# Softmax pass of a graph network: value minus last maximum by a second turning and a matmul with a negated identity on PE, in place of DVE's difference

## The reference, cut to what matters

```python
m = jax.nn.relu(feat[src]) + EPS
logits = BETA * m
seg_max = jax.ops.segment_max(logits, dst, num_segments=N)
ex = jnp.exp(logits - seg_max[dst])
denom = jax.ops.segment_sum(ex, dst, num_segments=N)
a = ex / denom[dst]
msg = jax.ops.segment_sum(a * m, dst, num_segments=N)
feats = feat + msg
return feats @ W + b
```

## Time and profile before

| | us |
|---|---|
| median of 3 runs | 5384.24 |
| profiled execution, its own time | 5342.66 |
| its span, first to last instruction | 5340.8 |
| PE busy (share of the span) | 3187.4 (60%) |
| DVE busy | 2666.4 (50%) |
| POOL busy | 2506.9 (47%) |
| ACT busy | 1564.4 (29%) |

### The profile page before, as it was taken

How to read it: one execution, slowest core, us unless ns; L and a number is a source line. 1 busy time by engine, 2 the same in 40 slices (tenths; PEclk the granted TensorE clock), 3 DMA queues, 4 the chain that set the end, 5 groups by cost and what they waited for, 6 DMA issues and landing times.

```text
span 5340.8 us, 69053 instructions
## 1 busy us (share of the span) xinstructions
PE 3187.4 (60%) x18737; PEld 2331.0 (44%) x18737; DVE 2666.4 (50%) x5882; ACT 1564.4 (29%) x3677; POOL 2506.9 (47%) x2580
## 2 busy tenths in 40 slices
PE   1555555553755555455455555311129999999999
PEld 0333333332633333333333334210017777778777
DVE  4888888886554555445454554700001154433333
ACT  1777777773222222222222222200000011111000
POOL 7666666664455565556556565777750000000000
PEclk9999999999966666666766676555559999999999
DMA  5565555653233344333344334200017756676776
GB/s 186 192 199 195 197 197 192 202 195 104 57 101 104 100 107 103 102 101 100 104 105 103 101 99 109 81 2 0 12 37 266 256 197 248 234 262 250 257 274 230
DMA packets 387448, 796.21 MB, mean 149 GB/s; under 512 B 207412, under 2 KB 264600, under 8 KB 361128
## 3 DMA queue, kind: packets, MB, share of 16 engines
q1 hardware_dynamic: 239330, 586.35, 32.8%
q0 software_dynamic: 82320, 90.28, 8.3%
q10 hardware_dynamic: 65718, 118.62, 5.8%
HBM read 581.03 MB, written 213.92 MB: 149 GB/s over the span
## 4 chain that ended last, share of the span: by engine, by line
PE 29%; issue 17%; another core or an unknown queue 14%; DVE 5%; ACT 3%; SPq 3%; DMA 1%; ACTq 1%; DVEq 0%; POOL 0%
PE ps L1166 17%; PE ps L1096 6%; SPq L633 2%; ACT ps L1215 2%; PE ps L920 1%; PE ps L927 1%; PE ps L926 1%; DVE area L1664 1%; DVE second L1629 1%; ACT out_ring L1239 1%; DMA attr<-attr_parts 1%; ACTq L1241 1%; ACT dump L1219 1%; PE ps L1049 1%
## 5 line engine op out<-in xcount | busy, mean ns | idle before, releaser
L779 POOL DMA_INDIRECT area<-relu_table,early x784 | 741.5, 946 | 400.6 <-issue 214.9
L938 PE MATMUL ps<-ident,area 96*128 96x96 f32 x2352 | 436.4, 353 | 801.5 <-issue 296.0
L779 POOL DMA_INDIRECT area<-src_table,early x784 | 752.7, 960 | 240.6 <-issue 237.9
L938 PEld LDWEIGHTS ps<-ident,area 96*128 96x128 f32 x2352 | 347.6, 210 | 926.6 <-issue 651.0
L1664 DVE TENSOR_TENSOR_SCAN area<-flags,area,ps 96x512 f32<-96x512 int8 x196 | 249.7, 1274 | 906.1 <-ACT dump L1219 732.8
L1166 PE MATMUL ps<-second,area 128*128 128x288 bf16 x5194 | 650.7, 286 | 0.2 <-DVE second L1811 0.2
L788 POOL DMA_INDIRECT adj<-copies_ring,cell_ring x392 | 390.0, 995 | 531.7 <-DVE cell_ring L1645 425.3
L1166 PEld LDWEIGHTS ps<-second,area 128*128 128x128 f16 x5194 | 508.3, 98 | 127.6 <-DVE second L1811 0.5
L1629 DVE SCALAR_TENSOR_TENSOR second<-second,area,ps 128x512 bf16<-128x512 f32 x784 | 538.6, 744 | 0.0
L920 PE MATMUL ps<-second,w_ef_scaled 96*96 96x512 f32 x392 | 307.0, 876 | 297.3 <-ACT second L1263 158.7
L1096 PE MATMUL ps<-early,area 128*128 128x288 bf16 x2401 | 327.5, 293 | 261.9 <-issue 261.9
(11 more groups left out here) (330 smaller groups left out, 4687.0 us busy)
## 6 DMA issues: line engine op xcount, KB each, us to landing
area<-adj SPq DMA_DIRECT2D x147, 1632.0 KB
area<-adj SPq DMA_DIRECT2D x55, 1568.0 KB
adj<-early SPq DMA_DIRECT2D x102, 816.0 KB
soft_sums<-out_ring ACTq DMA_DIRECT2D x196, 384.0 KB
second<-key_dram SPq DMA_DIRECT2D x98, 512.0 KB
area<-dst_table SPq DMA_DIRECT2D x784, 48.0 KB
sums<-out_ring ACTq DMA_DIRECT2D x196, 192.0 KB
second<-caps_dram SPq DMA_DIRECT2D x98, 192.0 KB
```

The lines of the kernel that those rows point to most:

```text
L779: pool.indirect_dma_start(out=src_rows[:, s, c % CH, :], out_offset=None, in_=gather_table[p], in_offset=bass.IndirectOffsetOnAxis(ap=src_ ...
L938: last = nc.tensor.transpose(ps[:, b, c * F:(c + 1) * F], r[:, (s * CH + c) * P:(s * CH + c + 1) * P], ident[0:F, 0:F])
```

## The change

PE now makes the difference. `rise` turns the tile a second time, into `DECAY_BANK` + s % 2, with four ordinary matmuls against the identity (the tile as the stationary operand), and then adds to it `diag_s` times `last_max`, where `diag_s` is the identity times -1, made once in the set-up. The last matmul counts `scored`. ACT reads the difference from PSUM instead of from `weight`: first the negative half (to `weight`), then the positive half in place, then the two exponentials. DVE's L1681 goes. POOL's gather into a slot is allowed by `scored` instead of `turned`, since the slot is read twice. PE waits once for `index_made` before its first tile.

```diff
@@ gather (POOL)
-                    wait(pool, e["turned"], t - RING + 1)
+                    wait(pool, e["scored"] if kind == SOFT else e["turned"], t - RING + 1)
@@ PE
+                def rise(u, s):
+                    t = u * RING + s
+
+                    wait(pe, e["summed"], t - 1)
+                    for c in range(CH):
+                        nc.tensor.matmul(ps[0:F, DECAY_BANK + s % 2, c * P:(c + 1) * P], src_rows[:, s, c, :], ident[:, :],
+                                         start=c == 0, stop=False)
+                    wait(pe, e["maxed"], t + 1)
+                    nc.tensor.matmul(bank(DECAY_BANK + s % 2, F), diag_s[:, :], last_max[:, s * TE:(s + 1) * TE],
+                                     start=False, stop=True).then_inc(e["scored"], 1)
+
                 def turn_and_project(u, s):
                     turn(u, s)
                     project(u, s)
+                    rise(u, s)
...
                 if kind == SOFT:
+                    pe.wait_ge(index_made, 1)
                     over_tiles(pe, turn_and_project, lambda u, s: two_before(turn_back, u, s))
@@ soften (ACT)
-                    rise, rose, sank = weight[:, s % 2, :], bank(DECAY_BANK + s % 2, F), weight[:, s % 2, :]
-                    nc.scalar.activation(rose, rise, ACT.Relu).then_inc(e["parted"], 1)
+                    rose, sank = bank(DECAY_BANK + s % 2, F), weight[:, s % 2, :]
+                    nc.scalar.activation(sank, rose, ACT.Relu, scale=-1.0).then_inc(e["parted"], 1)
                     act.wait_ge(e["parted"], 2 * t + 1)
-                    nc.scalar.activation(sank, rise, ACT.Relu, scale=-1.0).then_inc(e["parted"], 1)
-                    nc.scalar.activation(rose, rose, ACT.Exp, scale=-1.0)
+                    nc.scalar.activation(rose, rose, ACT.Relu).then_inc(e["parted"], 1)
+                    nc.scalar.activation(sank, sank, ACT.Exp, scale=-1.0)
                     act.wait_ge(e["parted"], 2 * t + 2)
-                    nc.scalar.activation(sank, sank, ACT.Exp, scale=-1.0).then_inc(e["expd"], 1)
+                    nc.scalar.activation(rose, rose, ACT.Exp, scale=-1.0).then_inc(e["expd"], 1)
@@ DVE
+            v.tensor_scalar(diag_s[:, :], ident[0:F, 0:F], -1.0, None, ALU.mult)
...
                     dve.wait_ge(e["maxed"], t + 1)
-                    v.tensor_tensor(weight[:, b, :], bank(b, F), last_max[:, s * TE:(s + 1) * TE], ALU.subtract)\
-                     .then_inc(e["scored"], 1)
```

## The result

The changed kernel takes 5645.75 us (median of 4 runs, 5633.12 to 5655.96) against 5387.34 us for the kernel before in the same comparison (4 runs, 5378.25 to 5393.46): a ratio of 1.0478, 95% interval 1.0462 to 1.0495. The prediction was 5325 us, faster, with a range up to 5475. The sign was wrong, and the time lies outside the range. The profiled execution took 5655.96 us.

A forecast was written before the change was run, and what follows sets the result against it. The bound was taken as a loop of DVE's work and PE's late completions. A late tile of 6.4 us and another of 4.3, taken as 11.0 for two, gave 59 us less: 5384 to 5325 us, range 5283 to 5475.

The forecast's parts named there:

- ACT's floor: Softmax pass: ACT's work back to back takes 5.29 us a tile and stays, so no tile can be shorter.
- DVE's tile: Softmax pass: without the difference (0.61 us), DVE's own work falls from 4.88 to 4.27 us a tile.
- PE's clock: Softmax pass: PE at 1.2 GHz rises to the upper level when kept busy; its work is then 3.1 us a tile.
- rival A: Slower: gaps in the softmax pass drop PE to 1.2 GHz, a tile there 7.3 us; 5441 to 5500 us; chance 0.34.
- PE's added work: PE, softmax pass: second turning (0.9 us) and matmul with minus one (1.10 us) are hidden at the upper clock level.
- POOL's release: Softmax pass: gather for tile t+4 released some 2.4 us later, hidden since its data are needed about 23 us later.
- The late completions: Softmax pass: PE's completions seen 2.8 us after their modelled end in every second tile, as before the change.
- One small reading of the loop: Softmax pass before the change: pace-setting loop over two tiles, copy and maximum 1.69 us from 622.90, ending at 634.45.
- The gain: Softmax pass: a tile falls from 5.81 to 5.5 us, 59 us less in all; chance of this forecast 0.42.
- Rival C: Softmax pass: PE stays at the upper level, completions come earlier; 5.29 us a tile, 5283 us in all; chance 0.10.
- The place: The change in time lies in the softmax pass; outside 114 to 1250 us it is at most 10 us.

The follow-up runs named there:

- e1: Changed kernel with the softmax pass's gathers left out after the first four tiles, on a chip with late completions: 5274.54 us against 5379.66 for the kernel before.
- e14: Changed kernel with POOL iotas of 0.80 us in place of gathers after the fourth tile, on a chip with late completions: 5226.36 us against 5345.97 for the kernel before.
- e17: Kernel before without the softmax pass's gathers after the first four tiles, on a chip with late completions: 5251.26 us against 5338.78 for the kernel before.
- e9: The changed kernel itself, run again on a chip without late completions: 4498.57 us against 4503.64 for the kernel before, ratio 0.999.
- e15: Changed kernel with gather released after the second turning and one ACT copy moved to DVE, chip without late completions: 4438.52 us against 4504.1 for the kernel before.
- e4: Kernel before with four unused fp32 identity matmuls added on PE in each softmax tile, on a chip with late completions: 5448.02 us, ratio 1.0128.
- e3: Kernel before with only POOL's gather release moved behind DVE's difference, on a chip with late completions: 5487.16 us, ratio 1.021.
- e13: Changed kernel with the gather released after the second turning, on a chip with late completions: 5462.02 us against 5345.97 for the kernel before, ratio 1.0218.
- e16: Kernel before without the softmax pass's gathers after the first four tiles, on a chip without late completions: 4502.09 us against 4504.1 for the kernel before.

## Why the prediction was wrong

**ACT's floor (right).** 5.29 us a tile, read from one pair of rows. Four programs that ran without held completions and with ACT's work unchanged (e1, e14, e17, e9) have 5.27 to 5.31, and e15, with less of it, 4.97.

**DVE's tile (right).** It was to fall from 4.88 to 4.27 us. On the second kind of chip DVE is busy 602.11 / 141 = 4.27.

**PE's clock (right about the rise, and rival A's mechanism is an effect rather than the cause).** L901 was to go from 659 to 410 ns. It takes 413 or 414 in all 141 cases on the second kind of chip, and in the change on the first kind 413 is the median. Before, the column said 1.00 at 659 ns, so that was missing data. In the change on the first kind the stretch's clock is 0.74, which seems to speak for A. But with the gathers gone the same program has 0.92 there (a window of e1, below) and with iotas 0.92 too. PE idles in the holes and does what follows at 1.2 GHz, as the 2.02 us of L939 at 710.12 show. That is a part of the loss, and an estimate bounds it: PE is busy 595.24 / 124 = 4.80 us a tile against 658.00 / 159 = 4.14 in e1, so 0.7 of the 1.9 us between them at most; 0.4 of it is L939 (198.9 / 124 against 194.7 / 159). A's 7.3 us for a tile at the lower level is close to 7.20 by chance; its own late tile, 8.4 us, came with 2.8 us of lateness and 4.2 for PE's work, and the real ones have some 6 and less.

```profile
300.00:1200.00 900.00, 658.00 (x3721) 407.60 (x3719) 714.20 (x716) 703.52 (x1610) 30.23 (x30) 0.92 0.45 171
```

**PE's added work (right on the second kind of chip, too low on the first).** The prediction let the second turning and the matmul with minus one be hidden at the upper clock. On the second kind they are: DVE waits 2.6 us for PE's turning in the whole pass. On the first kind e4 shows 68 us for four matmuls alone, with POOL's wait for a release at 1.45 us a tile instead of 0.94. That the cost comes by way of the release there too fits this wait, but isn't shown by it.

**POOL's release (the step that failed).** The prediction said of the gather's later release: "this is hidden unless landing took over 13 us". It asked only whether the gathered rows come in time, and they do (PE is never idle before L910). What it left out is that the release also sets *when POOL stops*, and that most held completions are let through only then. In e3 this step alone costs 107 us, where the sum had nothing for it; in e13 releasing earlier takes away a little over half of the loss.

**The late completions (the second step that failed, and it hangs on the first).** The sum took them "late by 2.8 in every second tile as now", a number that no row explained, and moved everything else around it. They are not a constant of the chip. They are a loop: completions are held, POOL runs out of released gathers, the completions come through, and only then can the work be done that releases POOL again. Before, that work was nothing: `turned` was itself one of the held completions, and POOL started within 0.3 us of DVE. The change puts into the loop the maximum and the matmul with minus one. In the timeline above POOL starts at 712.41, 3.6 us after DVE at 708.78. The prediction's last sentence said it would be wrong "if the late completions vanish or double". They doubled. (One small reading of the loop was off as well: the copy and the maximum take 1.50 us there, from 622.90 to 624.40, and not 1.69. The end of the loop, 634.45, was read directly and doesn't hang on it.)

**The gain (wrong for another reason on the second kind of chip).** There no completion is late, and the change gives 0.1%, inside what counted as no difference. The forecast's 59 us were to come out of DVE's waits, and DVE's waits were those for held completions. Where there are none, ACT is the bound in both kernels (5.31 us in e16, whose time is that of the kernel before, and 5.28), and DVE's saved 0.61 us turns into waiting for ACT (145.9 us before L1699 in e9's stretch, 1.03 us a tile). Rival C's 5.29 us was reached there, but the kernel before has it too.

**The place (partly right).** Of the 313 us between the profiled executions 276 lie in the softmax pass. The message pass, whose code is the same, took 1919.7 us by its scans (1748.8 to 3668.5) and before 1884.6 (1474.4 to 3359.0). The 35 us of difference are more than the 10 us that the prediction allowed outside the pass. PE's completions are held in that pass too (below), but no run looked into why it got longer.

## What to carry to other kernels

If several engines wait for one engine's completion and are let go together at a moment that its own work doesn't explain, the lateness is a loop to be found, not a constant to be kept in the sum: look for the engine that fell idle just before, and for the semaphore that changed last. A wait that is moved later must be priced by when its engine stops and starts again, and not only by when its data are needed. And time taken off an engine that waits part of the time is worth nothing until the one behind it (here ACT, known from one pair of rows) gives up work too.

## What the runs showed of the hardware

- On at least three chips PE's completions come up to 7 us after their modelled ends in a pass in which POOL issues indirect DMAs (136 of 383 in the change, median 6.1 us), and on two chips, with the same program, none does (0 of 564 in e9). With POOL's gathers replaced by iotas, or left out, they are on time on the first kind as well (0 of 601 in e14, 0 of 603 in e1). Not every completion under a gather is held: 116 of the 247 that were on time in the change came while one was being issued. What starts a hold, and what differs between the two kinds, stays open.
- A hold mostly ends when the gathers have stopped. In the change 112 of the 136 late counts came 1.0 to 2.3 us after the end of POOL's latest gather instruction, with a median of 1.8 for all of them; in e13 it is 159 of 181. In e3 it is 120 of 188, so it isn't the whole rule. In the hole above the last gather is issued by 706.99. The DMA engines in 40 slices of 0.3 us from 700 to 712 us:

```profile
DMA  4351013467999999998968410420000006995000
```

  The last activity is in the slices up to 708.1, then the engines are idle for some 1.8 us; ACT starts at 708.11 and DVE at 708.78. So in this hole PE's completions come through about when the last packets have moved, and not when POOL's last instruction ends. The Trainium skill, "Perfetto Trace Analysis", DMA Instruction — SWDGE (GPSIMD), says that the profiled end of such an instruction is the end of writing descriptors and not of moving data. The trace agrees: from 706.99 to 708.4 us it has 41 packets, all of the queue `software_dynamic`, which carries the gathers (15861 packets from 300 to 1200 us in the change, 1389 in e1).
- The two kinds of chips differ in the message pass too, whose code no experiment touched: its 196 scans take 1919.7 us in the change on the first kind and 1482.3 on the second (1331.2 to 2813.5). POOL gathers and scatters there. From 1800 to 2700 us 169 of the 224 counts by PE in the change's trace are late on the first kind (median 8.4 us), and none of 345 on the second.
